# The first weight chunk in two transfers, and one warming matmul fewer

## The reference

```
q = x @ Wq + bq                      # (16, 100, 512)
k = ctx @ Wk + bk                    # (16, 722, 512)
v = ctx @ Wv + bv
w = softmax(q @ k^T / sqrt(512), axis=1)     # over the 100 tokens
y = w @ v + x
out = (y - mean) * rsqrt(var + eps) * gamma + beta
```

## Time and profile before

| what | value |
|---|---|
| median of 3 runs | 146.08 us (145.47 to 146.15) |
| time of the profiled execution | 146.08 us |
| its span, first to last instruction | 144.3 us |
| TensorE busy | 135.2 us (94%), 1046 matmul instructions |
| VectorE busy | 113.2 us (78%) |
| ScalarE busy | 82.0 us (57%) |
| GpSimd busy | 65.2 us (45%) |
| mean granted TensorE clock | 0.996 |

### The profile page before, as it was taken

How to read it: one execution, slowest core, us unless ns; L and a number is a source line. 1 busy time by engine, 2 the same in 40 slices (tenths; PEclk the granted TensorE clock), 3 DMA queues, 4 the chain that set the end, 5 groups by cost and what they waited for, 6 DMA issues and landing times.

```text
span 144.3 us, 2969 instructions
## 1 busy us (share of the span) xinstructions
PE 135.2 (94%) x1046; PEld 130.3 (90%) x1046; DVE 113.2 (78%) x216; ACT 82.0 (57%) x286; POOL 65.2 (45%) x61
## 2 busy tenths in 40 slices
PE   6999999999999979999999999999999999999910
PEld 6998999998998969999999999999999999998900
DVE  0699979999777898658696976778696976786992
ACT  4587259559536927294756628484756627483520
POOL 1000000008032492716667553647577553649891
PEclk9999999999999999999999999999999999999998
DMA  4999999944076594796997979698887976645113
GB/s 113 384 417 417 420 289 368 343 152 183 5 222 236 195 336 176 262 397 212 305 331 251 363 233 391 234 321 316 291 305 230 370 252 195 225 124 194 73 73 145
DMA packets 10670, 37.33 MB, mean 259 GB/s; under 512 B 1184, under 2 KB 1184, under 8 KB 10656
## 3 DMA queue, kind: packets, MB, share of 16 engines
q1 hardware_dynamic: 9424, 34.92, 68.8%
q10 hardware_dynamic: 1232, 2.23, 4.1%
HBM read 33.87 MB, written 3.28 MB: 257 GB/s over the span
## 4 chain that ended last, share of the span: by engine, by line
PE 84%; POOL 4%; DVE 4%; ACT 3%; issue 2%; POOLq 1%; DVEq 0%; ACTq 0%
PE ps_U L400 26%; PE ps_S L386 25%; PE ps_Y L421 11%; PE ps_Y L361 6%; PE ps_U L361 6%; PE ps_Y L325 3%; POOL xT_in L848 2%; POOL xT_in L836 2%; ACT expo L521 2%; PE ps_w L409 1%; ACT xT_in L539 1%; PE ps_S L331 1%; DVE probsum L690 1%; PE ps_U L331 1%; PE ps_S L335 1%
## 5 line engine op out<-in xcount | busy, mean ns | idle before, releaser
L521 ACT ACTIVATE expo<-scores,negmax 121x100 f32<-121x100 f32 x96 | 35.1, 369 | 28.0 <-DVE negmax L679 28.0
L386 PE MATMUL ps_S<-G,ctxT_in 128*121 128x100 f32 (+1 forms) x384 | 43.5, 270 | 0.0
L400 PEld LDWEIGHTS ps_U<-prob,ctx_in 121*128 121x128 f32 x360 | 42.2, 192 | 0.9
L400 PE MATMUL ps_U<-prob,ctx_in 121*128 121x100 f32 x360 | 42.5, 274 | 0.0
L386 PEld LDWEIGHTS ps_S<-G,ctxT_in 128*121 128x121 f32 (+1 forms) x384 | 42.0, 185 | 0.0
L825 POOL TENSOR_TENSOR prob<-expo,rinv 121x600 f32<-121x600 f32 x16 | 19.0, 1190 | 35.6 <-DVE rinv L686 35.6
L841 POOL TENSOR_TENSOR rstd<-vareps,neg_half 128x1 f32<-128x1 f32 (+1 forms) x13 | 12.4, 956 | 23.4 <-DVE vareps L717 23.1
L836 POOL TENSOR_TENSOR xT_in<-x_in,xT_in 128x512 f32<-128x512 f32 (+1 forms) x13 | 16.6, 1278 | 13.5 <-issue 9.0
L690 DVE TENSOR_REDUCE probsum<-prob 121x100 f32<-121x600 f32 x16 | 19.8, 1238 | 2.5 <-POOL prob L825 2.2
L675 DVE TENSOR_TENSOR scores<-ps_S,c_rows 121x600 f32<-121x600 f32 x16 | 12.5, 781 | 11.3 <-issue 10.9
L521 ACT ACTIVATION_READ_ACCUMULATOR expo<-scores,negmax 121x1 f32 x96 | 18.2, 190 | 0.0
(11 more groups left out here) (91 smaller groups left out, 174.6 us busy)
## 6 DMA issues: line engine op xcount, KB each, us to landing
ctx_in<-ctx SPq DMA_DIRECT2D x16, 768.0 KB, 4.6
ctxT_in<-ctxT SPq DMA_DIRECT2D x16, 722.0 KB, 4.8
xT_in<-xT SPq DMA_DIRECT2D x8, 400.0 KB, 8.2
x_in<-x SPq DMA_DIRECT2D x12, 256.0 KB, 4.5
out<-xT_in ACTq DMA_DIRECT2D x8, 256.0 KB, 3.5
wqk<-Wqk SPq DMA_DIRECT2D x4, 388.0 KB, 4.5
out<-xT_in SPq DMA_DIRECT2D x3, 256.0 KB, 2.0
wv_in<-Wv SPq DMA_DIRECT2D x1, 512.0 KB, 16.1
```

The lines of the kernel that those rows point to most:

```text
L386: last = nc.tensor.matmul(ps_scores(c)[0:rows(c), :], ctxT_in[:, q, l * M + c * MP:l * M + c * MP + rows(c)], G[:, l, bass.ds(b * T, T)], ...
L400: last = nc.tensor.matmul(ps_U[:, q, l * T:(l + 1) * T], ctx_in[0:rows(c), q, c, l * P:(l + 1) * P], prob[0:rows(c), q, c * T:(c + 1) * T] ...
L521: last = nc.scalar.activation(expo[0:MP, q, c * T:(c + 1) * T], scores[0:MP, q, c * T:(c + 1) * T], ACT.Exp, bias=negmax[0:MP, q, c:c + 1] ...
```

## The change

The first chunk comes in two transfers: Wq's columns 256 to 511 with Wk and the biases (520 floats of each row), then Wq's columns 0 to 255. The first has a semaphore of its own. ScalarE makes the upper half of Wq's chunk 0 in two pieces, VectorE starts on Wk when the first transfer is in, and TensorE takes the four banks of each first group in the order 2, 3, 0, 1, with a wait for the second piece ahead of bank 0 of chunk 0. WARM goes from 9 to 8.

```diff
-        WARM = 9
+        WARM = 8
...
+            sp.dma_start(wqk[:, 0, E // 2:], Wqk[0, :, E // 2:]).then_inc(first_half_in, 16)
+            sp.dma_start(wqk[:, 0, 0:E // 2], Wqk[0, :, 0:E // 2]).then_inc(w_in[0], 16)
-            for c in range(EC):
+            for c in range(1, EC):
                 sp.dma_start(wqk[:, c, :], Wqk[c]).then_inc(w_in[c], 16)
...
                 wait_upper_wk(pe, f)
-                pe.wait_ge(wqhi_set, f + 1)
-                for e in range(EC):
+                if f == 0:
+                    pe.wait_ge(first_wqhi_set, 1)
+                else:
+                    pe.wait_ge(wqhi_set, f + 1)
+                for e in (2, 3, 0, 1):
+                    if f == 0 and e == 0:
+                        pe.wait_ge(wqhi_set, 1)
                     nc.tensor.matmul(banks[e][:, 0:L + 2], wq_hi[:, f, e * P:(e + 1) * P], wk_hi[:, f, :],
                                      start=(f == 0), stop=False)
...
             for f in range(EC):
-                act.wait_ge(w_in[f], 16)
-                if f > 0:
+                if f == 0:
+                    act.wait_ge(first_half_in, 16)
+                    nc.scalar.activation(wq_hi[:, f, E // 2:], wqT[:, f, E // 2:], ACT.Copy).then_inc(first_wqhi_set, 1)
+                    act.wait_ge(w_in[f], 16)
+                    nc.scalar.activation(wq_hi[:, f, 0:E // 2], wqT[:, f, 0:E // 2], ACT.Copy).then_inc(wqhi_set, 1)
+                else:
+                    act.wait_ge(w_in[f], 16)
                     nc.scalar.activation(wk_hi[:, f, :], wkT[:, f, :], ACT.Copy).then_inc(wkhi_set, 1)
-                nc.scalar.activation(wq_hi[:, f, :], wqT[:, f, :], ACT.Copy).then_inc(wqhi_set, 1)
+                    nc.scalar.activation(wq_hi[:, f, :], wqT[:, f, :], ACT.Copy).then_inc(wqhi_set, 1)
...
             for c in range(EC):
-                dve.wait_ge(w_in[c], 16)
                 if c == 0:
+                    dve.wait_ge(first_half_in, 16)
                     nc.vector.tensor_copy(wk_hi[:, c, :], wkT[:, c, :]).then_inc(first_wkhi_set, 1)
+                else:
+                    dve.wait_ge(w_in[c], 16)
                 wait_upper_wk(dve, c)
                 nc.vector.tensor_tensor(wk_lo[:, c, :], wkT[:, c, :], wk_hi[:, c, :].bitcast(F32), ALU.subtract).then_inc(wklo_set, 1)
+                if c == 0:
+                    dve.wait_ge(first_wqhi_set, 1)
+                    dve.wait_ge(w_in[c], 16)
                 dve.wait_ge(wqhi_set, c + 1)
                 nc.vector.tensor_tensor(wq_lo[:, c, :], wqT[:, c, :], wq_hi[:, c, :].bitcast(F32), ALU.subtract).then_inc(wqlo_set, 1)
```

More of the change, by code:

```diff
@@ L115, in xattn @@
         ps_c = ps("ps_c", [P, 512])
+        first_half_in = sem("first_half_in")
         w_in = [sem(f"w_in{c}") for c in range(EC)]
@@ L128, in xattn @@
         onesr_set = sem("onesr_set")
+        first_wqhi_set = sem("first_wqhi_set")
         wqhi_set = sem("wqhi_set")
```

## The result

| | before | after |
|---|---|---|
| median (15 runs each) | 145.99 us | 146.61 us |
| range of the runs | 145.40 to 146.33 | 146.06 to 147.39 |
| profiled execution: time, span | 146.08, 144.3 us | 146.61, 144.8 us |

The ratio is 1.0049, 95% interval 1.0036 to 1.0063: 0.5 to 0.9 us slower, where 0.2 us faster was forecast.

What follows compares the result with a forecast made beforehand. TensorE's path to `project(0)` was taken as the bound, with VectorE's chain close behind. TensorE's 0.25 us gain, cut to 0.15 to 0.2 by VectorE, was put at 0.2: 145.9 us, own range 145.6 to 146.1, ends 145.2 and 146.6.

Steps and rivals of the forecast that it cites:

- The failed step: Split's cost to later transfers: SP's issues 0.45 us later, hidden by full queue; 128 more packets cost 0.1 us.
- No wait there: TensorE in W: chunk 1 ready at 6.3, chunk 3's data in before TensorE reaches it at 9.9; no wait.
- VectorE's chain: First token group's rests to `W_lo`: transfer 0.1 later, so gain at most 0.15 us; bounds 0.25 and -0.05.
- The first transfer: Kernel start: 128 of 388 KB left for later, landing 0.3 us earlier, at 4.05; bounds 0 and 0.5.
- One warming matmul fewer: TensorE before W: two fewer warming pieces free 0.44 us at the low clock; next load possible at 4.47.
- The clock: TensorE's W stage: rise stays at 6.5, so W starts 0.5 us earlier but ends only 0.25 earlier.
- the later-clock rival: Rival, 10%: less warming work and a hole before W make the clock rise later; 146.4 to 147.1 us.
- The order 2, 3, 0, 1: TensorE's banks: bank 0 written again after two matmuls, not four; cost 0, bounds 0 and 0.02 us a matmul.
- "nothing": Rival, 17%: split costs the queue 0.3 us, 146.1 us, or first transfer lands no earlier, 146.0 us.
- the three signs of being wrong: First piece starting at 4.3 or later; clock changing other than at 6.5; TensorE's wait near 36 changing over 0.2 us.
- the wait near 36: At 35.95 TensorE waits 0.28 us for VectorE's L666; a change over 0.2 us would show the forecast wrong.

Runs made afterwards that it cites:

- e3: Kernel before, first chunk whole, with chunk 1 and everything behind it issued later, held by a 512-column memset on VectorE: ratio 1.0053.
- e10: Kernel before with only the split of the first chunk, all engines waiting for both halves, the second half issued by ScalarE: ratio 0.9992.
- e5: Changed kernel with the second half of chunk 0 issued by ScalarE instead of SP: ratio 0.9977.
- e2: Kernel before with eight warming matmuls for nine and nothing else: ratio 1.0002.
- e4: Changed kernel with nine warming matmuls, as in the kernel before: ratio 1.0039, median 146.52 us.
- e1: Kernel before with its first chunk in two transfers on SP and nothing else, every engine waiting for both: ratio 1.0044.
- e14: Kernel before with chunks 0 and 1 issued as before, chunk 2 and all behind it about 0.45 us later: ratio 1.0046.
- e8: Kernel before with chunk 1 and all behind it held back by two memsets, expected about 0.95 us later: ratio 1.0012.
- e6: Kernel before with chunk 1 issued by ScalarE at its start and the rest by SP: ratio 1.0034.

## Why the prediction was wrong

- **The failed step** is the sentence that SP issues everything behind 0.45 us later, "hidden as long as the queue is full, which it is from slice 2 on". The slice is 3.6 us wide, and the issues at stake feed the engines in its neighbourhood, while they are still starting. I had the finer row before me, 2.5 to 3.0 with a share of 0.79 and 199 GB/s, and used it only for the size of the first transfer. A 9 in the row isn't full speed either: in the hole of after, at 4 to 5 us, the share is 0.88 with 208 GB/s. Without the split, a later issue cost +0.53% (e3), and with the split but without the later issues nothing (e10). The other half of the same step, 0.1 us for 128 more packets, held: in e5 a packet took 122 ns in the median at 3104 bytes, 85 at 2080 and 46 at 1024, so two pieces cost 9 ns more than one, for eight packets of an engine 0.07 us.
- **Its consequences.** "No wait there" for chunks 1 to 3 fell with it: TensorE stood 0.82 us before chunk 1. The first token group came 0.82 later, where 0.1 was taken and 0.3 was the bound.
- **VectorE's chain** was the right mechanism and the one that priced the loss: 0.82 us of lateness less the 0.25 of idle before `W_lo` is 0.57; measured 0.50 at `W_lo`, at 36 us and in the span. I had used it only as a cap of a gain.
- **The first transfer** came earlier than taken, 3.54 for 4.05, the weight load at 4.49 for 4.58; the second piece was hidden, ready at 4.30 for a third matmul at 5.13. Right in sign and order. Part of it is luck of the profile: where chunk 0 came whole, and first by itself, it came at 3.91 to 4.35, and the profile before has the latest of these. That the edits of the engines are worth something shows only between e10 and e5 (0.9992 and 0.9977), and their intervals overlap.
- **One warming matmul fewer** costs and brings nothing that shows (e2, e4): ratio 1.0002, 0.9984 to 1.0019, which leaves room for some 0.2 us either way.
- **The clock** rose earlier in the profile after (two matmuls in 0.24 us from 5.55 on, for 6.55 before), so that the later-clock rival had no part in this profile. That it moved by a microsecond where 6.5 was taken as fixed was luck of the execution. It gained nothing: the matmuls of chunk 0 ended at 6.67 in place of the forecast's 7.0 or later, and the idle before chunk 1 was longer by as much. By the Trainium skill ("TensorE: Matmul & The Clock Gate", Part 1) the moment varies by half a microsecond between executions; here, over executions of different kernels, it varied more, see below.
- **The order 2, 3, 0, 1** was not tried by itself.
- **The rivals.** The nearest was "nothing", with 0.3 us for the queue; the slower one had the wrong mechanism. None let the transfers themselves slow down. Of the three signs of being wrong, only that of the clock was met; the wait near 36 grew by 0.17, under its 0.2, and none of them was on chunks 1 to 3.

The Trainium skill ("DMA: Bandwidth & Descriptors", Rules for kernel authors) says that spreading transfers over issuing engines brings no bandwidth and saves only issue time. e10 against e1 agrees: e10 moved 1468 KB from 3 to 7 us, before 1494, and the issue time of 0.45 us that it saved on SP was worth 0.5%.

Not shown is why, when chunks 2 and 3 are issued late, some parts of a chunk land up to 2 us after the others, though SP is by then transfers ahead. The records say that single packets took long, not for what they waited.

## What to carry to other kernels

A transfer that is split costs the issuing queue another issue, and everything behind it moves; at the start of this kernel no full queue hid that. So try the extra issue on an idle engine's queue, and look at the first transfers in half-microsecond stretches, not in slices. When an engine idles only a quarter microsecond before its critical step, ask of every transfer that feeds it how late it may come, in both directions. A gain at the head of one chain is worth nothing until the chain beside it gains too: here the span followed VectorE's `W_lo` and not TensorE's first matmul.

## What the runs showed of the hardware

- Chunks 2 and 3 issued 0.3 to 0.5 us late made the first token group 0.7 to 0.9 us late against the profile before, more than themselves (e3, e14, after), and 0.9 us no more than that (e8).
- In the losing kernels a transfer's 16 parts landed up to 2.1 us apart, with single packets of up to 1.3 us (e14) for a median of 0.12.
- The moment at which the clock rises from 1.2 to 2.4 GHz differs between profiles with no pattern in the kernels: near 4.0 in e14, 5.5 in after, 6.5 before, and in e3 near 7.3. TensorE had worked since 1.12 in all of them. In e3 its pairs show it, 0.42 and 0.27 us apart and then 0.24 (start us, us, engine, line):

```profile
6.85 0.62 PE L342 MATMUL ps_S<-wk_hi,wq_parts 128*128 128x258 f32 x2
7.27 0.43 PE L342 MATMUL ps_U<-wk_hi,wq_parts 128*128 128x258 f32 x2
7.54 0.41 PE L334 MATMUL ps_S<-wk_hi,wq_parts 128*128 128x258 f32 x2
7.78 0.40 PE L334 MATMUL ps_U<-wk_hi,wq_parts 128*128 128x258 f32 x2
```

- Two transfers on two queues share the engines, and the one that was first alone lands later: chunk 0 at 4.95 in e6, against 4.35 before and 3.91 in the earliest other profile.
